# A recommendation tower on one core: gathers tied to TensorE's progress, and pair products in a cyclic layout

## The reference

```python
def cin(inputs, W0, W1):                 # inputs: (b, 32 fields, 32 dims)
    x = inputs
    res = []
    for W in (W0, W1):
        prev = x.shape[1]
        z = einsum('bhd,bmd->bhmd', inputs, x).reshape(b, 32 * prev, 32)
        x = einsum('bpd,pj->bjd', z, W)  # 128 outputs
        res.append(x)
    return sum(concatenate(res, axis=1), axis=-1)

z = cin(e, W0, W1)                       # (1024, 256)
h = concatenate([z, dense_ctx], axis=1)  # + 16 columns
h = maximum(h @ W_top1 + b_top1, 0)      # 512
h = maximum(h @ W_top2 + b_top2, 0)      # 256
y = h @ W_top3                           # (1024, 1)
```

## Time and profile before

| | us |
|---|---|
| median of 3 runs | 377.18 (376.98 to 377.78) |
| span of the profiled execution | 597.7 |
| PE busy in it | 412.6 (69%) |
| POOL busy in it | 246.5 (41%), 256 gathers of 245.8 |
| ACT busy in it | 235.5 (39%) |
| DVE busy in it | 203.4 (34%) |
| TensorE's mean granted clock | 0.800 |

### The profile page before, as it was taken

One profiled execution on the slowest core, in us unless ns is written; L12 is line 12 of the kernel. 1 busy time (PEld: TensorE's weight loads), 2 busy tenths in 40 slices (PEclk: granted clock), 3 DMA queues, 4 the chain that ended last, 5 costly groups with the idle time before them and its releaser, 6 DMA issues.

```text
span 597.7 us, 9512 instructions
## 1 busy us (share of the span) xinstructions
PE 412.6 (69%) x3656; PEld 360.8 (60%) x3656; DVE 203.4 (34%) x834; ACT 235.5 (39%) x774; POOL 246.5 (41%) x262
## 2 busy tenths in 40 slices
PE   5512112874257887877788778687787679999988
PEld 4301001653256776766666667577676668989988
DVE  4200000694723333322333233333332235556510
ACT  3300000662175334522343334433452237676641
POOL 6777772547055444544445554544444440000000
PEclk9755555795589877877787888977787779999999
DMA  8100000000000000000000000000000000000000
GB/s 299 45 14 13 13 13 6 11 3 14 2 10 10 8 10 7 10 8 9 9 9 10 10 10 9 11 8 9 8 10 8 8 10 2 2 2 2 2 2 1
DMA packets 10765, 9.66 MB, mean 16 GB/s; under 512 B 4664, under 2 KB 8896, under 8 KB 10720
## 3 DMA queue, kind: packets, MB, share of 16 engines
q0 software_dynamic: 8192, 4.21, 4.8%
q1 hardware_dynamic: 2528, 4.84, 2.3%
HBM read 9.03 MB, written 0.00 MB: 15 GB/s over the span
## 4 chain that ended last, share of the span: by engine, by line
PE 57%; issue 18%; another core or an unknown queue 11%; DVE 7%; ACT 6%; DMA 1%; SPq 0%; ACTq 0%
PE WA L725 20%; PE QB L697 10%; PE PA L687 8%; PE T L710 4%; DVE RT L421 4%; PE M L738 4%; PE M L757 2%; PE ET L674 2%; ACT eblk L285 2%; ACT TS L285 1%; PE PA L639 1%; PE M L764 1%; PE M L748 1%; ACT RT L285 1%
## 5 line engine op out<-in xcount | busy, mean ns | idle before, releaser
L278 POOL DMA_INDIRECT emb<-in_table,rows x256 | 245.8, 960 | 239.0 <-PE ET L674 165.3
L725 PE MATMUL WA<-TS,RX 128*128 128x128 f32 x896 | 127.0, 301 | 1.0 <-ACT TS L285 1.0
L584 DVE COPY TS<-T 32x64 f32<-32x64 f32 x256 | 55.5, 217 | 200.6 <-PE T L710 184.6
L725 PEld LDWEIGHTS WA<-TS,RX 128*128 128x128 f32 x896 | 119.7, 215 | 6.0 <-issue 6.0
L697 PE MATMUL QB<-eblk,zQ 128*64 128x68 f32 x1024 | 69.1, 243 | 74.3 <-issue 74.0
L697 PEld LDWEIGHTS QB<-eblk,zQ 128*64 128x64 f32 x1024 | 49.9, 146 | 89.8 <-issue 85.8
L552 DVE TENSOR_TENSOR zQ<-ET,eT 128x1024 f32<-128x1024 f32 x32 | 39.2, 1225 | 159.0 <-ACT eT L285 158.9
L687 PE MATMUL PA<-eblk,zP 128*128 128x132 f32 x512 | 80.6, 296 | 5.3 <-issue 3.4
L639 PE MATMUL PA<-sym,TS 128*128 128x272 f32 x64 | 29.4, 552 | 74.5 <-issue 47.3
L687 PEld LDWEIGHTS PA<-eblk,zP 128*128 128x128 f32 x512 | 73.4, 212 | 6.3 <-issue 4.9
L285 ACT ACTIVATE eblk<-ET 32x256 f32<-32x256 f32 x128 | 48.6, 380 | 71.0 <-PE ET L674 66.0
(11 more groups left out here) (87 smaller groups left out, 294.1 us busy)
## 6 DMA issues: line engine op xcount, KB each, us to landing
emb<-in_table,rows POOLq DMA_INDIRECT x256
TS<-in_W SPq DMA_DIRECT2D x8, 256.0 KB, 4.3
wt<-in_W_top SPq DMA_DIRECT2D x2, 512.0 KB
y1w<-in_W_rows SPq DMA_DIRECT2D x1, 448.0 KB
TS<-in_W_rows SPq DMA_DIRECT2D x1, 448.0 KB
sym<-in_W_cols SPq DMA_DIRECT2D x1, 264.0 KB, 2.8
TS<-in_W_cols SPq DMA_DIRECT2D x1, 264.0 KB, 3.1
idc<-in_ids SPq DMA_DIRECT2D x1, 128.0 KB, 2.0
```

Of the source, the lines that this page charges most:

```text
L278: eng.indirect_dma_start(emb[par][:, g, :], None, table, bass.IndirectOffsetOnAxis(rows[:, k, g:g + 1], 0))\
L584: eng.tensor_copy(view(ts[32 * q:32 * q + 32, :, :], P * REST + b0, [[4 * P, 2], [P, 4], [1, 8]]), view(src, q, [[C17, 2], [4, 4], [C33, 8 ...
L725: m = eng.matmul(WA[:, 0:P], C[:, kt, :], TS[k % 2][:, slot_of(kt), :], start=(kt == 0), stop=(kt == KT - 1))
```

## The change

Three things are changed.

1. Gathers are numbered n = 0 to 255. The first 16 go as before. Gather n from 16 to 27 waits until `rt_made` is 2(n - 16) + 9. From n = 28 on every second gather waits: with u and j the quotient and remainder of (n - 28) / 8, the first two pairs of gathers and the third wait for trio 0, 1 and 2 of unit u, the fourth pair for the unit's third bank (`t3_made`). The old wait for `et_made` stays.
2. The pairs within a block of 8 fields are laid out cyclically: distance s and distance 8 - s share 8 places. With a copy `eT` that holds 12 fields for each block (the 8, and the first 4 again), the products of distances 1 to 3 are one DVE instruction of 24 x 32 numbers, distance 4 and the squares one of 8 x 32. Five DVE instructions for a unit take the place of eleven. The order of pairs in `RT`, and so the columns of the weights, follows the same layout.
3. ACT writes `eT` in two instructions (8 fields and 4 fields for each block), ahead of the four of `eblk`.

The core of the diff:

```diff
+TURN = SUB + SUB // 2
+FREE = 16
+PACED = 28
 def off(s):
-    return sum(SUB - r for r in range(1, s))
+    return SUB * (s - 1) if s <= SUB // 2 else SUB * (SUB - 1 - s) + s
...
-    NZ = 11
+    NZ = 5
...
+            def gate(n):
+
+                if FREE <= n < PACED:
+                    eng.wait_ge(rt_made, 2 * (n - FREE) + SUB + 1)
+                elif n >= PACED and n % 2 == 0:
+                    u, j = divmod(n - PACED, UG)
+                    if j // 2 < TRIOS:
+                        eng.wait_ge(p_made, TRIOS * u + j // 2 + 1)
+                    else:
+                        eng.wait_ge(t3_made, u + 1)
+
             eng.wait_ge(rows_made, 1)
             for k in range(TILES):
                 par = k % 2
                 for unit in range(UNITS):
                     wait(eng, et_made, UNITS * (k - 2) + unit + 1)
                     for g in range(UG * unit, UG * unit + UG):
+                        gate(UG * UNITS * k + g)
                         eng.indirect_dma_start(emb[par][:, g, :], None, table,
...
+                parts = ET[:, 0:GROUPS * F].rearrange("p (g i) -> p g i", i=SUB)
+                copy(eT[:, :, 0:SUB], parts).then_inc(eblk_made, 1)
+                copy(eT[:, :, SUB:], parts[:, :, 0:TURN - SUB]).then_inc(eblk_made, 1)
                 for v in range(NQ):
...
-                copy(eT[:, :], ET[:, 0:GROUPS * F]).then_inc(eblk_made, 1)
...
                 if part == 1:
-                    for s in range(1, 5):
-                        apart(s)
+                    turns = SUB // 2 - 1
+                    eng.tensor_tensor(view(within, 0, [[32, parts], [SUB, turns], [1, SUB]]),
+                                      field(0, [[SUB, parts], [0, turns], [1, SUB]]),
+                                      copied(1, [[TURN, parts], [1, turns], [1, SUB]]), ALU.mult).then_inc(z_made, 1)
                 if part == 2:
-                    for s in range(5, SUB):
-                        apart(s)
-                    some = [[SUB, parts], [1, 4]]
-                    eng.tensor_tensor(view(within, PAIRS, [[32, parts], [1, 4]]), field(0, some), copied(0, some),
-                                      ALU.mult).then_inc(z_made, 1)
+                    eng.tensor_tensor(view(within, off(4), [[32, parts], [4, 2], [1, 4]]),
+                                      field(0, [[SUB, parts], [0, 2], [1, 4]]),
+                                      copied(4, [[TURN, parts], [-4, 2], [1, 4]]), ALU.mult).then_inc(z_made, 1)
```

More of the change, by code:

```diff
@@ L108, in dlrm_cin_tower @@
         emb = [sb(f"emb{i}", [P, P // NQ, D]) for i in range(2)]
-        eT = sb("eT", [P, GROUPS * F])
+        eT = sb("eT", [P, GROUPS * NQ, TURN])
         eblk = [sb(f"eblk{i}", [P, GROUPS, NQ, 2 * C17]) for i in range(2)]
@@ L536, in copied @@
             def copied(a, dims):
-                return view(eT[:, :], a, dims)
+                return view(eT[:, :, :], a, dims)
             def products(u, part):
@@ L542, in products @@
                 within, across, rest = zP[u % 2][:, :, :], zQ[u % 2][:, :, :, :], z3[u % 2][:, :, :]
-                def apart(s):
-                    some = [[SUB, parts], [1, SUB - s]]
-                    eng.tensor_tensor(view(within, off(s), [[32, parts], [1, SUB - s]]), field(0, some), copied(s, some),
-                                      ALU.mult).then_inc(z_made, 1)
                 if part == 0:
-                    eng.wait_ge(eblk_made, (NQ + 1) * (u + 1))
+                    eng.wait_ge(eblk_made, (NQ + 2) * (u + 1))
                     wait(eng, t3_made, u - 1)
@@ L553, in products @@
                                       field(0, [[HALF, sides], [1, SUB], [0, SUB]]),
-                                      copied(SUB, [[HALF, sides], [0, SUB], [1, SUB]]), ALU.mult).then_inc(z_made, 1)
+                                      copied(TURN, [[2 * TURN, sides], [0, SUB], [1, SUB]]), ALU.mult).then_inc(z_made, 1)
                 if part == 1:
-                    for s in range(1, 5):
-                        apart(s)
+                    turns = SUB // 2 - 1
+                    eng.tensor_tensor(view(within, 0, [[32, parts], [SUB, turns], [1, SUB]]),
+                                      field(0, [[SUB, parts], [0, turns], [1, SUB]]),
+                                      copied(1, [[TURN, parts], [1, turns], [1, SUB]]), ALU.mult).then_inc(z_made, 1)
                 if part == 2:
-                    for s in range(5, SUB):
-                        apart(s)
-                    some = [[SUB, parts], [1, 4]]
-                    eng.tensor_tensor(view(within, PAIRS, [[32, parts], [1, 4]]), field(0, some), copied(0, some),
[L563 to L566, removed]
+                    eng.tensor_tensor(view(within, off(4), [[32, parts], [4, 2], [1, 4]]),
+                                      field(0, [[SUB, parts], [0, 2], [1, 4]]),
+                                      copied(4, [[TURN, parts], [-4, 2], [1, 4]]), ALU.mult).then_inc(z_made, 1)
+                    eng.tensor_tensor(view(rest, 0, [[THIRD, GROUPS], [4, 4], [1, 4]]),
+                                      field(4, [[F, GROUPS], [SUB, 4], [1, 4]]),
+                                      copied(4, [[NQ * TURN, GROUPS], [TURN, 4], [1, 4]]), ALU.mult).then_inc(z_made, 1)
                     eng.tensor_copy(view(rest, MORE, [[THIRD, GROUPS], [1, HALF]]), field(0, [[F, GROUPS], [1, HALF]]))\
```

## The result

| | before | after |
|---|---|---|
| median of 12 runs each, us | 377.25 (376.6 to 380.47) | 380.29 (379.0 to 382.34) |
| ratio after to before | | 1.0084, 95% interval 1.0062 to 1.0106 |
| span of the profiled execution, us | 597.7 | 378.5 |
| granted clock in it | 0.800 | 0.973 |

The change costs 3.0 us. The prediction said slower, by 5.5 us.

A forecast was written before the change was run, and what follows sets the result against it. The prediction took POOL's rate of gathers as the bound: gather 255 at 328.7 + 3 + 41.0 = 372.7 against 367.2, so +5.5 us on 377.18 gives 382.7. Its own range was 379 to 386, with the rivals 370 to 388.

The forecast's parts named there:

- The bound: Whole kernel: without the recorded execution's waits, POOL's rate of gathers bounds it, eight taking 9.98 us against PE's 9.08.
- The ten microseconds around the span: Outside the kernel's span: 10.0 us left between POOL's 367.2 us and the timed median of 377.18.
- POOL's chain: Gathers at 1.248 us each to gather 255 at 323.2, then 3 and 41.0 us to the end: 367.2 us.
- PE's chain: PE's work from front to end without waits: 85.5 + 24.0 + 217.9 + 34.0 = 361.4 us.
- The cost of the gates: Front: gather 60 waits for trio 12, starting at 85.3 instead of 79.8; cost 5.5 us, never caught up.
- The gates ahead of these: Front, gathers 16 to 27: step 30 ends at 37.1, before gather 27 would start at 38.6; cost 0.
- The waits of the recorded execution: Recorded execution: its 220 us of waits are hardly in timed runs; the span falls because gathers can't pile up.
- Products: DVE's products: 0.4 us less a unit, a set 2.7 instead of 3.1 us; weights in the front 1.2 us earlier.
- `eT` in two instructions: ACT's extra instruction: 0.2 us once in the front, later hidden by PE but for 0 to 0.3 us a tile.
- PE as the bound: Rival: PE's chain decides if a gather takes below 1.19 us; 376.2 to 378.2 us; 0.19 together with gates not binding.
- Real waits: Rival: timed runs have some of PE's waits during gathers, which spreading removes; 371.4 us, down to 366; chance 0.29.
- Gates that don't bind: Rival: trio 12 comes before 79 us, POOL runs as before, 377 us; 0.19 together with PE as the bound.

The follow-up runs named there:

- e4: Kernel before with every second gather of tiles 4 to 7 left out; 369.48 us, ratio 0.9796.
- e2: Changed kernel without the gates, so the layout alone; 377.69 us, ratio 1.0011.
- e5: Kernel before, unchanged, recorded once more with a profile; 378.79 us, span 377.0.
- e10: Kernel before with every second gather of tiles 4 to 7 left out, run again beside e9 on the same chip; 369.30 us, ratio 0.9793.
- e9: Changed kernel without its gates and with every second gather of tiles 4 to 7 left out; 372.73 us, ratio to before 0.9854.
- e1: Kernel before with the gates alone, products and eT as before; 380.93 us, ratio 1.0095.
- e8: Kernel before with the work behind the last tile's gathers reordered for a shorter tail; 374.98 us, ratio 0.9929.
- e3: Changed kernel with the gated gathers 24 later (FREE 40, PACED 52 for 16, 28); 378.24 us, ratio 1.0019.
- e6: Changed kernel with each of DVE's sums of the front replaced by a set to zero; 373.24 us, one run.

## Why the prediction was right, and where it was not

**The bound: right.** POOL's row of gathers sets the end, before and after: e4 without half of the late gathers is 7.7 us quicker. The tail of 43.6 us (forecast 3 + 41.0 = 44.0) and the pitch of 1.248 us hold: from 91.39, 195 gathers of 1.248 make 334.75, and 334.90 was measured.

**The ten microseconds around the span: wrong.** The prediction had POOL's chain at 367.2 us and put the 10.0 us that were left around the span. Only 1.8 lie there. The Trainium skill (Runtime: NRT & Kernel Launch, "The ~15µs preamble/postamble breakdown") gives 9 to 15 us, into which the 10.0 fitted. The times of these runs hold 1.75 to 1.88 us besides the span, and the measurement decides; whether the parts that the page lists lie outside the measured time no run shows. The rest was in POOL's chain itself: the sum held every gather of the front at 0.94 us, and those beside DVE's sums take up to 2.74. Gather 60 without gates starts at 88.67 and not at 79.8. With that, 367.2 + 8.9 - 0.4 = 375.7, which is e2's span, and with 1.8 it is 377.5, its median but for 0.2. The recorded execution of before hid most of it, since POOL rested through much of DVE's sums there, but not all: behind a rest, one gather in POOL's timeline of before takes 4.13 us while the sums from 117.29 to 130.74 run. The working looked at the mean and at two rows and passed it over.

```profile
127.54 4.13 POOL L278 DMA_INDIRECT emb<-in_table,rows  x1 [11.91 <-PE ET L674]
131.97 0.94 POOL L278 DMA_INDIRECT emb<-in_table,rows  x1 [0.30 <-issue]
```

Two errors of 8 us cancelled in the total, which is luck, and a residue that fits a page was taken for confirmation.

**PE's chain: short by 5.8 us.** Trio 12 starts at 90.28 in after, where the working had 84.5. Two steps failed. The products of the front start at 31.74 and not at 29.1: the sum of steps at 0.89 us left out the first unit's transposes, where PE waits for gathers and then for ACT. From after's timeline of PE:

```profile
18.99 0.44 PE L685 MATMUL ET<-ident,emb 128*128 128x128 f32 x2 [1.94 <-DMA emb<-in_table,rows]
...
22.04 0.73 PE L650 MATMUL PA<-sym,TS 128*128 128x272 f32 x2 [0.83 <-ACT RT L300]
```

And from the first weights to trio 12 it takes 90.28 - 71.33 = 18.95 us instead of 15.5. The working had taken the waits of 3.13 and 2.31 us out as the recording's. At the same two places after has waits of its own, for ACT's copies of the weights:

```profile
71.33 1.12 PE L676 MATMUL M<-ident,RT 128*128 128x128 f32 x4 [6.64 <-DVE QC L437]
...
79.72 1.10 PE L676 MATMUL WA<-ident,RT 128*128 128x128 f32 x4 [2.61 <-ACT RX L300]
...
84.52 0.66 PE L676 MATMUL M<-ident,QC 128*128 128x128 f32 x4 [0.93 <-ACT RX L300]
```

So 3.5 of the 5.4 us that were taken out are the kernel's (3.2 in e5, the kernel before, where these waits are 2.44 and 0.75). "issue" as the reason of a wait did not mean that nothing real was behind it. Between these points the working was good: from 34.47, where the sums begin, to 71.27, where the last ends, it is 36.8 us, and 37.8 less two gains of 0.4 was forecast. In e4 and e10, which have before's layout and in which PE sets the end, trio 12 starts at 90.50 and 90.94 where the working had 85.5; with these 5.0 to 5.4 us more PE's chain is 366.4 to 366.8, and their spans are 366.8 and 367.3.

**The cost of the gates: right in kind, 2.7 for 5.5.** The term of the sum was the distance between POOL's own arrival at gather 60 and the end of trio 12. Both moved: POOL's arrival by 8.9 us, the trio by 5.8. What was held of 5.5 is 5.5 - 8.9 + 5.8 = 2.4; the 0.3 that are left are the time from a trio's end to the gather that it lets go (85.50 + 0.62 = 86.12 to 86.39), which the working put at nothing. That the two errors go the same way is luck: each is larger than the whole cost. With POOL's alone the gates would have cost nothing, with PE's alone 11 us. The gate at which POOL stands is gather 56's on trio 11, not gather 60's on trio 12, but the two come to the same: trio 12 ends at 91.12 and would have let gather 60 go at 91.39, when it starts anyway.

The gates ahead of these, put at 0, are not idle: gathers 23 to 28 wait up to 1.16 us, 2.5 us in all above the 0.30 of every gather, and at gather 47 POOL is 1.2 us behind e2. By the times they add nothing, since gather 56 has to wait for trio 11 in any case. That the gates after trio 12 are open when POOL comes, and that the loss is never caught up, came out as forecast.

**The waits of the recorded execution: right that they are not in the timed runs, wrong in why they would go.** The prediction said that the profiled span would fall because gathers that follow PE can no longer pile up. It fell, but e2 and e5 fall the same without gates. For the waits being the recording's own the prediction cited the Trainium skill's rule that the trace block holds its producers back (NOTIFIC — the notification-queue block, 7.1); no run here shows that, and no other recorded execution, with gates or without, has such waits.

**Products: right.** One set of after, in DVE's timeline, from 31.74 to the first sum at 34.47, is 2.73 us (2.7 forecast, 3.1 before):

```profile
31.74 1.22 DVE L563 TENSOR_TENSOR zQ<-ET,eT 128x1024 f32<-128x1024 f32 x1 [7.32 <-ACT eblk L300]
32.88 0.95 DVE L568 TENSOR_TENSOR zP<-ET,eT 128x768 f32<-128x768 f32 x1
33.75 0.41 DVE L572 TENSOR_TENSOR zP<-ET,eT 128x256 f32<-128x256 f32 x1
...
34.27 0.28 DVE L578 COPY z<-ET 128x128 f32<-128x128 f32 x1
```

**`eT` in two instructions: wrong, without consequence.** "Hidden by PE but for 0 to 0.3 us a tile" came from ACT's share of busy time. It is 0.14 us in every unit, since ACT's copies end last there, those of the third bank in three units of a tile and `h` in the fourth. POOL covers it in this kernel; where it doesn't (e9), the layout loses 3.9 us behind the front, and 3.4 in the medians. In the front, where the working had 0.2 us for it, PE waits 0.83 us for ACT behind the first unit's transposes in after and 0.68 in e1, which has the old `eT`: 0.15.

**The rivals.** PE as the bound is out (e4, e8 and the table). Real waits are out (e5 and the spans of the timed runs). Gates that don't bind are what e3 is, not this change.

## What to carry to other kernels

When one engine runs an unbroken row of equal work to the end of the kernel, whatever holds it up early is paid in full at the end, and a lead given up in the front can't be bought back; look for the point from which it never waits again, and count only the delay there and the tail behind its last piece. Before a remainder is put down to what lies around the span, find where the span and the time of one and the same run stand; and before a wait is deducted as an artefact, look whether a second recording has it at the same place. A busy share says little about whether one more instruction is hidden: what counts is which engine ends last at the point where the others wait.

## What the hardware showed that I had not expected

- A gather's 0.94 us on POOL is not fixed: beside DVE's additions or copies from SBUF to SBUF it took up to 7.01 us, 8.0 us in all in after. Which gather is hit varies from run to run with the same instructions. In e5, with the same additions, one gather took nearly three times as long as in after:

```profile
44.94 5.18 DVE L421 TENSOR_TENSOR RT<-RT,RX 128x112 f32<-128x112 f32 x24
44.97 5.89 POOL L278 DMA_INDIRECT emb<-in_table,rows  x1 [0.30 <-issue]
```

The 7.01 us in e3's run of 382.65 us, against a median of 378.24, are the same. The last gather starts 1.4 us later in e5 than in e2, and 5.2 us later in e3.

- TensorE's granted clock in after is 0.61 on average from 56 to 71 us, with PE waiting 6.64 us for DVE up to 71.33, and 0.70 from 71 to 85.5. The weights take 1.1 us there for four matmuls that take 0.66 later. In e6, where PE's longest wait from 50 to 85 us is 3.71 us, the clock is 0.98 and 0.90. The two stretches of after:

```profile
56.00:71.00 15.00, 6.77 (x66) 5.87 (x66) 14.65 (x65) 5.99 (x21) 11.95 (x11) 0.61 0.08 11
71.00:85.50 14.50, 10.63 (x55) 9.85 (x55) 5.05 (x16) 10.34 (x29) 10.53 (x11) 0.70 0.10 14
```

- One profiled execution lay 220 us above every other run of the same kernel, with the same pitch of gathers within its bursts. A single profile can be an outlier by far more than the differences that it is read for.
